# A two-layer attention block on one core: k'v in column groups of one head, greatest k on VectorE, and the large buffers laid out anew at multiples of 2 KB

## The reference

```python
xn = layernorm(x)                                   # over the 512 columns
q, k, v = xn @ Wq + bq, xn @ Wk + bk, xn @ Wv + bv  # three 512x512 weights
k = where(masked row, -inf or -1e6, k);  v = where(masked row, 0, v)
q = softmax(q, over the columns of a head)
k = softmax(k, over the 512 rows of a batch)        # greatest k by column is subtracted
attn = k.T @ v          # by head: 32x32 (layer 0) or 64x64 (layer 1)
y = q @ attn            # layer 0 uses attn turned: einsum('bhtd,bhed->bhte', q, attn)
h = layernorm(y) * (1 + scale) + shift              # scale, shift from silu(cond) @ W_film
x = x + silu(h) @ W_out + b_out
```

## Time and profile before

| | |
|---|---|
| median of 3 runs | 976.93 us |
| lowest, highest | 976.09, 977.97 us |
| the profiled execution | 976.61 us, with a span of 974.6 us and a mean granted clock of 0.996 |
| PE busy, PEld busy | 949.1 us (97%), 794.9 us (82%) |
| DVE, ACT, POOL busy | 589.8 (61%), 402.8 (41%), 278.8 us (29%) |
| instructions | 14227, of them 5082 matmul records |

### The profile page before, as it was taken

The page is one execution under the profiler, slowest core; times in us unless marked ns, Lnnn a source line. Parts: engine busy times, 40 slices in busy tenths (PEclk is TensorE's granted clock), DMA queues, the critical chain, the costliest instruction groups (busy, mean ns, idle before and its releaser), DMA issues.

```text
span 974.6 us, 14227 instructions
## 1 busy us (share of the span) xinstructions
PE 949.1 (97%) x5082; PEld 794.9 (82%) x5082; DVE 589.8 (61%) x1215; ACT 402.8 (41%) x611; POOL 278.8 (29%) x308
## 2 busy tenths in 40 slices
PE   4999999999999999999999999999999999999987
PEld 3778888888888888887888888888888888888875
DVE  5666746656565565755777665565755656565563
ACT  5335344442533534344363544425344433533522
POOL 2022423304242131423124333042422304242230
PEclk9999999999999999999999999999999999999999
DMA  7543030120303003031440301203030120302002
GB/s 230 214 153 130 1 130 0 43 86 0 129 0 117 12 5 124 0 130 60 176 175 1 141 1 47 83 0 129 0 129 0 43 86 0 129 0 114 16 1 87
DMA packets 19610, 71.22 MB, mean 73 GB/s; under 512 B 3392, under 2 KB 3448, under 8 KB 13440
## 3 DMA queue, kind: packets, MB, share of 16 engines
q1 hardware_dynamic: 19584, 70.88, 19.1%
HBM read 54.10 MB, written 16.78 MB: 73 GB/s over the span
## 4 chain that ended last, share of the span: by engine, by line
PE 95%; DVE 3%; issue 1%; ACT 0%; POOL 0%; POOLq 0%; SPq 0%; DVEq 0%; ACTq 0%
PE psum_w L368 54%; PE psum_k L368 18%; PE psum_k L553 5%; PE psum_k L591 5%; PE psum_t L581 3%; PE psum_t L431 3%; PE psum_t L418 3%; PE psum_t L526 1%; PE psum_t L395 1%; DVE y L896 0%; DVE x_in L658 0%; DVE y L766 0%; PE psum_k L563 0%; PE psum_t L531 0%; PE psum_t L404 0%
## 5 line engine op out<-in xcount | busy, mean ns | idle before, releaser
L1042 POOL TENSOR_TENSOR xT_low<-xT,xT_high 128x512 fp32r<-128x512 f32 x60 | 77.3, 1288 | 236.1 <-ACT xT_high L948 234.7
L971 ACT ACTIVATE gate<-psum_t,film_shift,film_scale 128x512 f32<-128x512 f32 x64 | 49.7, 777 | 143.2 <-PE psum_t L431 113.2
L1034 POOL TENSOR_SCALAR x_var<-x_moments 128x4 f32<-128x4 f32 x16 | 3.7, 229 | 367.7 <-DVE x_moments L652 359.8
L368 PE MATMUL psum_k<-w_high_k,xT_high 128*128 128x512 f32 x256 | 105.0, 410 | 0.5 <-DVE y L896 0.5
L368 PE MATMUL psum_w<-w_high_v,xT_high 128*128 128x512 f32 x256 | 103.7, 405 | 0.1
L368 PE MATMUL psum_w<-w_high_q,xT_high 128*128 128x512 f32 x256 | 101.5, 396 | 0.0
L368 PE MATMUL psum_w<-w_high_v,xT_low 128*128 128x512 f32 x256 | 101.1, 395 | 0.0
L368 PE MATMUL psum_k<-w_high_k,xT_low 128*128 128x512 f32 x256 | 101.1, 395 | 0.0
L368 PE MATMUL psum_w<-w_low_q,xT_high 128*128 128x512 f32 x256 | 101.0, 395 | 0.0
L368 PE MATMUL psum_w<-w_high_q,xT_low 128*128 128x512 f32 x256 | 101.0, 395 | 0.0
L368 PE MATMUL psum_w<-w_low_v,xT_high 128*128 128x512 f32 x256 | 100.9, 394 | 0.0
(11 more groups left out here) (126 smaller groups left out, 1924.3 us busy)
## 6 DMA issues: line engine op xcount, KB each, us to landing
x_in<-x_between_layers SPq DMA_DIRECT2D x9, 1024.0 KB, 4.8
x_res<-in_x SPq DMA_DIRECT2D x8, 1024.0 KB, 6.8
x_between_layers<-x_res SPq DMA_DIRECT2D x8, 1024.0 KB, 3.9
x_in<-in_x SPq DMA_DIRECT2D x7, 1024.0 KB, 4.8
x_res<-x_between_layers SPq DMA_DIRECT2D x7, 1024.0 KB, 6.8
out_x<-x_res SPq DMA_DIRECT2D x7, 1024.0 KB, 3.9
raw_weights<-in_L_cond_film_emb_W SPq DMA_DIRECT2D x4, 1024.0 KB, 6.2
raw_weights<-in_L_cond_W_emb SPq DMA_DIRECT2D x4, 1024.0 KB, 5.1
```

What stands on the lines that cost most here:

```text
L368: mm = pe.matmul(bank, lhs[:, c, rows_of_tile], rhs[w][:, c, :], start=(c == 0 and n == 0), stop=(c == CHUNKS - 1 and n == 2))
L971: act.activation(gate[:, c % 2, :], psum_t[:, c % 2, :, :].rearrange("p t s -> p (t s)"), ACT.Silu, scale=film_scale[:, cond, c:c + 1].rea ...
L1042: pool.tensor_tensor(xT_low[:, c, :], xT[:, c % 2, :], xT_high[:, c, :], ALU.subtract)\
```

## The change

Four things are changed at once.

1. **Greatest k without PE.** The four transposes of `k_max` on PE, the matmul that spreads the shift, and ACT's copy of it are gone. DVE turns `k_max` in blocks of 32x32 (`turn_k_max`), reduces it, joins the four groups of 32 partitions by copies and maxima on 128x16 elements, adds and subtracts the bias of k, and turns the result back with a broadcast input into `k_shift_rows` (`k_shift_of`). The bias of k comes in eight small DMAs from an array that holds the same values in another order.
2. **k'v by head.** For each chunk and tile there is a matmul for each head: in layer 0 four with 32 columns of `k_exp` stationary and 34 columns of `v` moving, in layer 1 two with 64 and 66. Each writes the partitions of its own head, that is, its own column group of the array. `v` holds the two mask columns once for each head. The output is 4 x 34 or 4 x 66 columns of `psum_k[:, 0]`.
3. **The attention blocks** are made on 4 x 32 or 4 x 64 columns, not on 4 x 128. In layer 0 DVE turns them in four block transposes, and `turn_att` on PE and the copy back are gone. `head_blocks` and `v_bias_blocks` are gone.
4. **The layout.** Small tables that are declared first fill up to a multiple of 2048 bytes, and then come all large buffers (`w_high` to `bias_o`), each with a size that is a multiple of 2048. `xT_high` and `gT_high` now lie a multiple of 2048 from `w_high_q`.

The diff, cut to its core:

```diff
-        w_high = [sb(f"w_high_{n}", [P, CHUNKS, DIM], F32R) for n in "qkvo"]
...
+        minus_half = sb("minus_half", [P, TILES])
+        w_high = [sb(f"w_high_{n}", [P, CHUNKS, DIM], F32R) for n in "qkvo"]
+        w_low = [sb(f"w_low_{n}", [P, CHUNKS, DIM], F32R) for n in "qkvo"]
+        xT_high = sb("xT_high", [P, CHUNKS, SEQ], F32R)
+        xT_low = sb("xT_low", [P, CHUNKS, SEQ], F32R)
+        gT_high = sb("gT_high", [P, CHUNKS, SEQ], F32R)
+        gT_low = sb("gT_low", [P, CHUNKS, SEQ], F32R)
+        raw = sb("raw_weights", [P, 2 * CHUNKS, DIM])
+        k_exp = sb("k_exp", [P, TILES, DIM])
...
+        def head_view(tile, layer, extra=0):
+
+            n = DIM // HEADS[layer] + extra
+            return tile[:, 0:CHUNKS * n].rearrange("p (g n) -> p g n", n=n)
+
+        def v_of(layer):
+            n = DIM // HEADS[layer] + SUMS
+            return v[:, :, 0:HEADS[layer] * n].rearrange("p t (h n) -> p t h n", n=n)
+
+        def att_psum_of(layer):
+            return head_view(psum_k[:, 0, :], layer, SUMS)
...
                 v_projection(0)
                 v_projection(1)
 
-                pe.wait_ge(k_max_done, TILES * (i + 1))
-
-                if with_output:
-                    pe.wait_ge(gate_ready, CHUNKS * (i - 1) + 3)
-                else:
-                    pe.wait_ge(xT_ready, CHUNKS * i + 3)
-                for c in range(CHUNKS):
-                    mm = pe.transpose(psum_t[:, 0, c, :], k_max[:, c * P:(c + 1) * P], ident[:, :])
-                mm.then_inc(k_max_turned, 1)
                 v_projection(2)
-
-                pe.wait_ge(k_shift_ready, i + 1)
-                pe.matmul(psum_t[:, 0, :, :].rearrange("p c n -> p (c n)"), ones[:, :],
-                          k_shift[:, :, :].rearrange("p c n -> p (c n)"), start=True, stop=True)\
-                  .then_inc(k_shift_spread, 1)
                 v_projection(3)
...
                 for g in range(CHUNKS):
                     for t in range(TILES):
-                        mm = pe.matmul(att_psum[:, g, 0:VCOLS], k_exp[:, t, g * P:(g + 1) * P], v[:, t, g, :],
-                                       start=(t == 0), stop=(t == TILES - 1))
+
+                        for h in range(P // width):
+                            of_head, at = slice(h * width, (h + 1) * width), g * P + h * width
+                            mm = pe.matmul(att_psum_of(layer)[of_head, g, :], k_exp[:, t, at:at + width],
+                                           v_of(layer)[:, t, g * (P // width) + h, :],
+                                           start=(t == 0), stop=(t == TILES - 1))
                 mm.then_inc(att_done, 1)
...
-                def turn_att():
-
-                    pe.wait_ge(att_built, i + 1)
-                    for g in range(CHUNKS):
-                        mm = pe.transpose(att_turned_psum[:, g, :], att_of[layer][:, g, 0:P], ident[:, :])
-                    mm.then_inc(att_turned, 1)
-
                 def turn_q(t):
                     pe.wait_ge(q_exp_ready, TILES * i + t + 1)
 
                     if t == 0:
-                        pe.wait_ge(k_shift_rows_ready, i + 1)
+                        if with_output:
+                            pe.wait_ge(gate_ready, CHUNKS * (i - 1) + 3)
+                        else:
+                            pe.wait_ge(xT_ready, CHUNKS * i + 3)
...
-                if layer == 0:
-                    turn_att()
...
+            def turn_k_max(i):
+                dve.wait_ge(k_max_done, TILES * (i + 1))
+                dve.transpose(k_turned[:, :, :].rearrange("p b r -> p (b r)"), k_max[:, :]).then_inc(k_max_turned, 1)
+            def k_shift_of(i, layer):
+                of_quad, other_half, of_half, other_quad, of_all, shift = (k_top[:, n, :] for n in range(6))
+                steps = K_TOP_STEPS * i
+                half = P // 2
+                dve.wait_ge(k_max_turned, i + 1)
+                dve.tensor_reduce(of_quad, k_turned[:, :, :], AX_X, ALU.max).then_inc(k_top_step, 1)
+                dve.wait_ge(k_top_step, steps + 1)
+                dve.tensor_copy(other_half[0:half, :], of_quad[half:P, :]).then_inc(k_top_step, 1)
+                dve.tensor_copy(other_half[half:P, :], of_quad[0:half, :]).then_inc(k_top_step, 1)
+                dve.wait_ge(k_top_step, steps + 3)
+                dve.tensor_tensor(of_half, of_quad, other_half, ALU.max).then_inc(k_top_step, 1)
+                dve.wait_ge(k_top_step, steps + 4)
+                for to in range(P // QUAD):
+                    frm = to ^ 1
+                    dve.tensor_copy(other_quad[to * QUAD:(to + 1) * QUAD, :], of_half[frm * QUAD:(frm + 1) * QUAD, :])\
+                       .then_inc(k_top_step, 1)
+                dve.wait_ge(k_top_step, steps + 8)
+                dve.tensor_tensor(of_all, of_half, other_quad, ALU.max).then_inc(k_top_step, 1)
+                dve.wait_ge(k_top_step, steps + 9)
+                if fixed(i, 0):
+                    dve.wait_ge(bias_k_loaded, 16 * LAYERS * (P // QUAD))
+                dve.tensor_tensor(of_all, of_all, bias_k[:, layer, :], ALU.add).then_inc(k_top_step, 1)
+                dve.wait_ge(k_top_step, steps + 10)
+                dve.tensor_tensor(shift, bias_k[:, layer, :], of_all, ALU.subtract).then_inc(k_top_step, 1)
+                dve.wait_ge(k_top_step, steps + 11)
+                dve.transpose(k_shift_rows[:, :].rearrange("p (b r) -> p b r", r=QUAD),
+                              shift.unsqueeze(2).to_broadcast([P, BLOCKS, QUAD])).then_inc(k_shift_rows_ready, 1)
...
                 if with_output:
-                    for c in range(CHUNKS):
-                        split_gate(i - 1, c)
+                    split_gate(i - 1, 0)
+                turn_k_max(i)
+                if with_output:
+                    split_gate(i - 1, 1)
+                k_shift_of(i, layer)
+                if with_output:
+                    split_gate(i - 1, 2)
+                    split_gate(i - 1, 3)
                 if fixed(i, 0):
                     greatest_masks(0)
 
-                dve.wait_ge(k_max_turned, i + 1)
-                dve.tensor_reduce(k_top[:, 0, :], psum_t[:, 0, :, :], AX_X, ALU.max).then_inc(k_top_step, 1)
-                dve.wait_ge(k_top_step, 3 * i + 1)
-                bias_k = params[:, layer, BK:BK + CHUNKS]
-                dve.tensor_tensor(k_top[:, 1, :], k_top[:, 0, :], bias_k, ALU.add).then_inc(k_top_step, 1)
-                dve.wait_ge(k_top_step, 3 * i + 2)
-                dve.tensor_tensor(k_top[:, 2, :], bias_k, k_top[:, 1, :], ALU.subtract).then_inc(k_top_step, 1)
-                dve.wait_ge(k_top_step, 3 * i + 3)
-                dve.tensor_tensor(k_shift[:, :, :], ident[:, :].unsqueeze(1).to_broadcast([P, CHUNKS, P]),
-                                  k_top[:, 2, :].unsqueeze(2).to_broadcast([P, CHUNKS, P]), ALU.mult)\
-                   .then_inc(k_shift_ready, 1)
...
-                dve.tensor_copy(att_sums[:, :, :], att_psum[:, :, P:VCOLS]).then_inc(att_step, 1)
+
+                att_sum, weighted = att_psum_of(layer), head_view(k_turned[:, :, :].rearrange("p b r -> p (b r)"), layer)
+
+                def of_row(col):
+                    return col.unsqueeze(2).to_broadcast([P, CHUNKS, width])
+
+                if fixed(i, layer * BATCHES):
+                    dve.wait_ge(bias_v_loaded, 16 * sum(HEADS[n] // CHUNKS for n in range(layer + 1)))
+                    dve.wait_ge(att_zeros_ready, ATT_ZERO_PIECES)
+                dve.tensor_copy(att_sums[:, :, :], att_sum[:, :, width:width + SUMS]).then_inc(att_step, 1)
                 dve.wait_ge(att_step, ATT_STEPS * i + 1)
-                dve.reciprocal(att_scale[:, 0, :], att_sums[:, :, 0]).then_inc(att_step, 1)
+                dve.tensor_tensor(weighted, head_view(bias_v, layer), of_row(att_sums[:, :, 1]), ALU.mult)\
+                   .then_inc(att_step, 1)
+                dve.reciprocal(att_scale[:, :], att_sums[:, :, 0]).then_inc(att_step, 1)
                 dve.wait_ge(att_step, ATT_STEPS * i + 2)
-                dve.tensor_tensor(att_scale[:, 1, :], att_scale[:, 0, :], att_sums[:, :, 1], ALU.mult)\
-                   .then_inc(att_step, 1)
-                for g in range(CHUNKS):
-                    dve.scalar_tensor_tensor(out=att[:, g, 0:P], in0=att_psum[:, g, 0:P],
-                                             scalar=att_scale[:, 0, g:g + 1], in1=head_blocks[layer][:, :],
-                                             op0=ALU.mult, op1=ALU.mult).then_inc(att_step, 1)
-                dve.wait_ge(att_step, ATT_STEPS * (i + 1))
-                for g in range(CHUNKS):
-                    mm = dve.scalar_tensor_tensor(out=att[:, g, 0:P], in0=bias_v[:, g, :],
-                                                  scalar=att_scale[:, 1, g:g + 1], in1=att[:, g, 0:P],
-                                                  op0=ALU.mult, op1=ALU.add)
-                mm.then_inc(att_ready if layer else att_built, 1)
```

(25 more changed lines are left out.)

141 lines of the change are left out of this document (70 added, 71 removed).

## The result

| | before | changed |
| --- | --- | --- |
| median of the runs | 976.66 us (976.09 to 977.97, 4 runs) | 927.16 us (926.00 to 928.24, 4 runs) |
| ratio | | 0.949, 95% interval 0.948 to 0.951 |
| span of the profiled execution | 974.6 us | 924.5 us |
| first start of k'v in iteration 0 | 55.35 us | 52.75 us |
| from the k'v of one iteration to the next, layer 0 (mean of 1 to 5) | 58.19 us | 54.27 us |

The time fell by 49.5 us. The forecast was 939.0 us, so the sign and most of the size were right, and the saving was 12 us larger than the 37.9 I had summed. The time lies in the stated range of 923 to 960 us, but under my own case of 930 to 950. The page of the changed kernel answers the earlier trace rows: PE is busy for 52 us less and still holds 97% of the span, and DVE has 9 us more work.

A forecast was written before the change was run, and what follows sets the result against it. PE was taken as the bound, busy 97% of the span, its time a sum of distances between matmul starts. Savings of 10.7 + 3.5 + 12.7 + 11.0 = 37.9 us off 976.61 gave 938.7, as median 939.0 us; range 923 to 960.

The forecast's parts named there:

- my own case: The whole kernel takes 930 to 950 us; chance 0.56.
- The layout: All 3072 L368 matmuls read operands at new places: taken as 0 us, likely reach -9 to +3.
- layout faster: L368 matmuls all at o's pace or better: 930 us and below; chance 0.13.
- Greatest k off PE: Four transposes and the spreading matmul leave PE in each of 16 iterations: 16 x 0.67 = 10.7 us saved.
- Attention blocks: In layer 0 four PE transposes go, 8 x 0.44 = 3.5 us saved; DVE's new steps taken as equal.
- k'v: k'v by head saves 1.82 us an iteration in layer 0 (12.7 us), 1.37 in layer 1 (11.0 us).
- the rival at 952 us: k'v gains little in layer 0, one record every 25 ns or more; chance 0.17 together with 969 us.
- The one at 969 us: k'v's heads run wholly one after the other, term -6.4 us; chance 0.17 together with 952 us.
- The sequencer's 62 ns and 988 us: PE's sequencer takes 62 ns for each short k'v record, 26 us lost against 14.2 won: 988 us; chance 0.05.
- The bound by DVE: o of tile 2 waits for DVE's first residual: layer 0 gives at most 0.25 us an iteration more.
- swallowed for k'v only: In iteration 0 PE's 2.15 us wait for DVE swallows k'v's saving, so layer 0's counts seven times.
- The granted clock: Clock falls to 0.50 in each iteration, 26 us in all: 965 us; chance 0.03.

The follow-up runs named there:

- the timed pair: Changed kernel with its buffers at the places of the kernel before, 940.11 us, against the changed kernel, 927.16 us.
- the second experiment: Changed kernel with its buffers put back at the places of the kernel before: 940.11 us, ratio 0.962 to the kernel before.
- the third experiment: Changed kernel with k'v's loops exchanged, all four tiles of one head and then the next head: 941.70 us, ratio 0.964 to the kernel before.
- the first experiment: Kernel before with only its buffers declared in the changed kernel's order: 968.21 us against 976.51, ratio 0.991.
- the last kernel of the study: Changed kernel with, in iteration 0, the copy of the condition's rows ahead of the attention chain and 7 unread filler products on PE: 922.83 us.

## Why the prediction was right in sign and short in size

The account of the two profiled executions, from the starts of k'v: the first comes 2.6 us earlier; iteration 0 to 1 gives 0.5; five of layer 0 give 5 x 3.92 = 19.6; the last two of that layer, with the condition's products of layer 1, 3.9 and 3.1; seven of layer 1 give 19.3; the tail 1.2. That is the 50.1 us by which the span fell, but for rounding.

**The layout is the term that failed.** I took 0 us with a reach of -9 and +3, and it measured 0.68 to 0.76 us an iteration, 11 us in all, 13.0 in the timed pair: outside that reach too. The step that failed is "the rows lie near the middle and differ by 4 ns, so I take 0". The rows held the answer half: two relations with two paces are a reason to think that the relation matters and that a third, where both start alike, may be better than either. I extrapolated to both sides evenly, though 228.7 was the one nearer to an even place (nearness alone is not the rule either: 32 and 64 bytes took 233.3). The rival "layout faster", 930 us and below, had 0.13 and was the case that came. By the rule of the Trainium skill that I had weighed ("TensorE: Matmul & The Clock Gate", "Step-by-step: what each phase is for"), by which loading the next weights takes nothing from the running matmul, the place would be worth nothing, as I read it; the runs, with 226.7 and 233.3 ns for one program at two relations of its operands, don't agree. Whether it is the load and the stream that collide, or something else, no run here shows.

**Greatest k off PE: right.** 0.67 us an iteration by the earlier trace rows, 11.2 us more with 10.7 put back. DVE in iteration 5 (start, duration, line, shape):

```profile
304.19 0.70 DVE L765 STREAM_TRANSPOSE k_turned<-k_max 128x512 f32<-128x512 f32 x1
...
306.71 0.76 DVE L782 COPY k_top<-k_top 32x16 f32<-32x16 f32 x4
...
308.14 0.72 DVE L794 STREAM_TRANSPOSE k_shift_rows<-k_top 128x512 f32<-128x512 f32 x1
...
309.95 2.48 DVE L864 TENSOR_TENSOR k_exp<-psum_k,k_shift_rows 128x512 f32<-128x512 f32 x4
```

A block transpose takes 0.70 to 0.72 us, my 0.7, and the chain from the first to the end of the second 308.86 - 304.19 = 4.67 us with a step of 0.65 for the gate between them: 4.0 for my 4.1. The additions end at 312.43, 13 us ahead of k'v.

**Attention blocks: right.** L563 is gone with its 0.44 us, and DVE's work on the blocks takes 2.45 us for 2.69. No run tests this part alone, but with it the iteration of layer 0 without the layout adds up: 0.67 + 0.44 + 2.14 = 3.25 us, and the second experiment has 3.24.

**k'v: right in layer 1 by luck, a little short in layer 0.** Layer 1: 1.36 us saved, 1.37 forecast, but two misses cancel in it. The records took 2.02 us where I had 1.85, and the changes of form 2.21 - 2.02 = 0.19 where I had 0.35. Layer 0: 2.14, forecast 1.82. I had let PE's sequencer bind, 22 ns for each of 64 instructions, 1.4 us; the 128 records took 1.26 in all, under 20 ns an instruction and 9.8 ns a record, and the changes of form 1.43 - 1.26 = 0.17 for my 0.35. For the rival at 952 us I had taken the Trainium skill's 25 ns from start to start ("TensorE: Matmul & The Clock Gate", "Wait — 56ns, not 53.3ns?") as a price of each record. That does not hold here, neither across groups (9.8 ns) nor within one (21 ns, the third experiment); taken as a price of each instruction, which leaves two records, it fails across groups alone (19.7 ns). With it that rival fell. The one at 969 us had taken 3.9 and 4.1 us a visit for one head after the other; in that order (the third experiment) the records took 2.70 and 2.64. The sequencer's 62 ns and 988 us fell too. Its mark of 45 ns a record was off in itself: by the same sums, a loss of 8 x (156 r + 0.70 - 7.14) us with r in us, a record must cost some 53 ns before the 14.2 us of the other parts are lost. For 0.32 us in six or seven iterations layer 0 brought 2 us.

**The bound by DVE was wrong.** I said that layer 0 can't give over 0.25 us an iteration more, as o of tile 2 waits for the first residual. k'v gave 0.32 more, and there is still no wait (the layout's 0.68 lies almost all outside the way from k'v to o of tile 2 and so does not count against this bound):

```profile
329.36 0.15 DVE L892 COPY att_sums<-psum_k 128x8 f32<-128x8 f32 x1
...
331.81 1.28 DVE L814 TENSOR_TENSOR x_res<-x_res,psum_w 128x512 f32<-128x512 f32 x2
```

The first of the two additions ends some 0.7 us behind 331.81, at 332.5, 7.1 us after the start of k'v and not 7.8, and PE comes at 332.98 for it. I had held the end of DVE's chain fixed to k'v's start. But the copy of the sums starts 329.36 - 325.36 = 4.0 us behind it instead of 4.4, and the chain from `att_sums` to the addition is 2.45 instead of 2.69 us. Why the steps ahead of the copy got shorter is open.

**What was given back, and chance.** The 37.9 of the forecast, 11 of the layout and 2 of k'v would be 51. Iteration 0 to 1 gave 0.5 us instead of 0.67 + 0.44 + 0.7 = 1.8, as PE waited longer for DVE's copy (3.3 us for 2.15) and stayed at the lower clock twice as long (6.8 us for 3.4). The longer wait need not be the cause of the longer low stretch, since the first experiment had 6.8 us behind a wait of 2.15. Moving the copy gave 2.9 us back (ratio 0.946 for 0.949, with intervals that lie apart). That a faster PE waits longer there I had swallowed for k'v only, and had not looked at what the clock does behind the wait. The first k'v came 2.6 us earlier, of which 0.7 is greatest k: the rest is the wait for the parameters' DMA, 10.7 us for 12.3, and it was 10.9 to 13.1 in the other profiled executions, so it is the luck of one. The granted clock never fell in a steady iteration, and that rival is out.

## What to carry to other kernels

Where PE is the bound and its time is a sum of start distances, compare the distances of matmuls that differ only in the buffers they read; if they differ, the relation of the two operands' addresses is a lever, and one pad tests it (here 0 modulo 256 bytes, 6 ns of 233, 1.4% of the kernel). Narrow blocks on a diagonal were cheaper as records of their own (2.70 us for 3.49 in layer 0), and cheaper still when neighbours in the order went to different column groups (1.26 us). And after a gain on PE, look at the few places where it already waited: there part of the gain can be given back, as waiting and as lower clock.

## What the runs showed of the chip that I had not expected

- An fp32r matmul of 128x512 starts every 226.7 ns when its two operands lie 0, 256 or 1024 bytes apart (modulo 2048), every 232.6 to 233.0 at 128 or 896, 233.3 to 233.4 at 32, 64 and 224, 228.7 to 228.8 at 1984.
- fp32 records of 34 columns (two to an instruction) start 9.8 ns apart in four alternating column groups and 21 ns apart in one; of 66 columns 31 ns in two groups, 41 in one.
- The granted clock fell to 0.50 behind a standstill of PE of 3.2 us and stayed at 1.00 when products filled it, but it also fell once behind 4.8 us in which PE was busy 4.61 (the last kernel of the study). What decides is open.
- In k of tile 0 one distance late in the tile is 300 to 345 ns in iterations 2 to 7 and 9 to 15 of every kernel of this study, whatever the layout. Why is open; with its neighbours it is worth 1.5 to 2 us in all.
